# Projections and cluster products of a clustered-attention stage, from one f32 product to three products of f16 parts

## The reference

```python
x = layernorm(inputs, ln1_g, ln1_b)
q = einsum('bsd,dhf->bshf', x, Wq)            # 16 heads of 8 features; k, v alike
qb = softmax(einsum('bshf,hfn->bshn', q, Whq))   # 32 clusters per head; kb alike
kb = softmax(einsum('bshf,hfn->bshn', k, Whk))
logits = einsum('bqhf,bkhf->bhqk', q, k) / sqrt(8)
logits = logits + 0.1 * einsum('bqhn,bkhn->bhqk', qb, kb)
out = einsum('bhqk,bkhf->bqhf', softmax(logits), v)
out = einsum('bqhf,hfd->bqd', out, Wo)
```

## Time and profile before

| what | value |
|---|---|
| median of 3 runs | 1559.28 us (1555.27 to 1565.25) |
| the profiled execution's own time | 1561.78 us |
| span of the profiled execution, first to last instruction | 1559.7 us |
| granted TensorE clock, mean | 0.941 |
| busy share over the span: PE, DVE, ACT, POOL | 84%, 74%, 66%, 50% |

### The profile page before, as it was taken

The page is one execution under the profiler, slowest core; times in us unless marked ns, Lnnn a source line. Parts: engine busy times, 40 slices in busy tenths (PEclk is TensorE's granted clock), DMA queues, the critical chain, the costliest instruction groups (busy, mean ns, idle before and its releaser), DMA issues. The chain is left out here.

```text
span 1559.7 us, 27015 instructions
## 1 busy us (share of the span) xinstructions
PE 1302.9 (84%) x9156; PEld 604.5 (39%) x9156; DVE 1154.4 (74%) x1983; ACT 1032.9 (66%) x2355; POOL 787.6 (50%) x957
## 2 busy tenths in 40 slices
PE   3488989999899886786899999859778999998596
PEld 1122222222222221572555555533235555555243
DVE  5778878888888772234888888859458888887493
ACT  3246666666666665775889999852268899987422
POOL 4567666676675500225767777500077667774000
PEclk9569999999999999897999999979889999999698
DMA  3523333333433300101111111010011111110001
GB/s 97 108 55 62 62 68 62 72 61 58 75 62 63 67 2 1 54 1 38 25 25 27 30 25 25 19 44 0 14 32 25 25 25 25 32 25 12 1 1 55
DMA packets 161259, 60.87 MB, mean 39 GB/s; under 512 B 139706, under 2 KB 152932, under 8 KB 161124
## 3 DMA queue, kind: packets, MB, share of 16 engines
q1 hardware_dynamic: 161124, 59.15, 18.0%
HBM read 8.66 MB, written 2.10 MB: 7 GB/s over the span
## 5 line engine op out<-in xcount | busy, mean ns | idle before, releaser
L633 DVE TENSOR_REDUCE row_max<-max_ps 128x2 f32<-128x1024 f32 x256 | 312.9, 1222 | 71.0 <-PE max_ps L445 69.6
L685 ACT ACTIVATE prob<-scores_ps 128x1024 f32<-128x1024 f32 x256 | 262.0, 1023 | 148.4 <-PE scores_ps L425 144.9
L1668 POOL TENSOR_TENSOR la_turned<-la_raw,lw_rot 128x1024 f32<-128x1024 f32 x64 | 150.7, 2355 | 275.6 <-ACT la_raw L1560 146.0
L1549 ACT ACTIVATE la_s<-la_s,la_bias,la_inv 128x128 f32<-128x128 f32 x512 | 222.9, 442 | 8.2 <-DVE la_bias L1462 7.9
L1305 PE MATMUL la_ring<-lw_wqkv,la_hT 128*128 128x512 f32 x384 | 205.7, 647 | 24.8 <-ACT la_hT L1544 13.4
L425 PE MATMUL scores_ps<-stack 128*128 128x512 f16 x512 | 155.8, 386 | 41.5 <-ACT prob L685 40.8
L1674 POOL TENSOR_TENSOR la_turned<-la_turned,la_swapped 128x1024 f32<-128x1024 f32 x64 | 150.6, 2353 | 5.0
L459 PE MATMUL heads_ps<-prob,v_pad 128*32 128x512 f32 x1024 | 137.3, 608 | 1.1 <-ACT prob L685 1.1
L445 PE MATMUL max_ps<-stack 24*128 24x512 f16 x512 | 102.8, 398 | 31.8 <-DVE row_max L633 19.2
L1437 DVE TENSOR_TENSOR la_swapped<-la_ring,lw_rot 128x256 f32<-128x256 f32 x256 | 92.0, 416 | 32.6 <-ACT la_raw L1560 25.3
L425 PEld LDWEIGHTS scores_ps<-stack 128*128 128x128 f16 x512 | 34.2, 97 | 208.5 <-ACT prob L685 160.8
(11 more groups left out here) (170 smaller groups left out, 2727.3 us busy)
## 6 DMA issues: line engine op xcount, KB each, us to landing
la_v_back<-la_v_own SPq DMA_DIRECT2D x112, 128.0 KB, 2.3
X<-in_x SPq DMA_DIRECT2D x8, 256.0 KB, 5.0
stack<-stack_tok SPq DMA_TRANSPOSE x128, 3.2
out<-X SPq DMA_DIRECT2D x8, 256.0 KB, 2.4
lw_wqkv<-in_wqkv SPq DMA_DIRECT2D x2, 768.0 KB, 4.9
stack<-shift_row SPq DMA_DIRECT2D x64, 2.0 KB
lw_rot<-in_rot SPq DMA_DIRECT2D x2, 512.0 KB, 6.2
lw_w<-in_fw SPq DMA_DIRECT2D x2, 341.0 KB
```

The costliest lines, as they stand in the source:

```text
L633: nc.vector.tensor_reduce(row_max[:, grp % 2, w // 2, :, w % 2], max_ps[:], AX.X, ALU.max).then_inc(max_made, 1)
L685: nc.scalar.activation(prob[:, c % 4, 2 * pr:2 * pr + 2, :], scores_ps[:], ACT.Exp, scale=1.0 / LOGIT_SCALE).then_inc(exp_made, 1)
L1549: ins = nc.scalar.activation(s_ps[:, place(h), :], s_ps[:, place(h), :], ACT.Exp, bias=bias[:, T % 2, h:h + 1], scale=inv[:, T % 4, h:h + ...
L1668: nc.gpsimd.tensor_tensor(spun, raw[:, T % 2].rearrange("p s (h f) -> p s h f", f=LD), rot[:, T % TPB, :, 0, :].unsqueeze(2).to_broadcast( ...
```

## The change

For the 28 tiles after the first batch the three products `qkv`, `clk` and `clq` are made of f16 parts: x_hi W_hi + x_hi W_lo + x_lo W_hi, accumulated in one PSUM bank, in place of one f32 product. What was issued for it:

- once, ScalarE copies `w_qkv` (384 columns) and `w_cl` (1024 columns) to f16, in the slot in which tile 1 is in step 0 (slot -41), ahead of everything else in that slot
- once, VectorE subtracts to get the low parts of both, in the slot in which tile 2 is in step 0 (slot -33), ahead of everything else in that slot
- for each of the 28 tiles, `turn_input` runs a second activation on the same bench region, with f16 output, before the one that writes `xnT`
- for each of them GpSimd subtracts `xnT_hi` from `xnT` (`split_input`, step -5, slot 2 modulo 8), after `scale_input` and ahead of `place_values` and the cluster work of that slot
- TensorE waits for `xnT_split` before each of the products, and once for the low weights

```diff
+            def project(out, x, whole, hi, lo):
+
+                if x < TPB:
+                    return nc.tensor.matmul(out, xnT[:, x % 2, :], whole, start=True, stop=True)
+                pe.wait_ge(xnT_split, x + 1 - TPB)
+                if x == TPB:
+                    pe.wait_ge(w_lo_made, 2)
+                nc.tensor.matmul(out, xnT_hi[:, x % 2, :], hi, start=True, stop=False)
+                nc.tensor.matmul(out, xnT_hi[:, x % 2, :], lo, start=False, stop=False)
+                return nc.tensor.matmul(out, xnT_lo[:, x % 2, :], hi, start=False, stop=True)
...
-                    mm = nc.tensor.matmul(bench[:, 0:3 * D], xnT[:, x % 2, :],
-                                          w_qkv[:].rearrange("p a b -> p (a b)"), start=True, stop=True)
+                    mm = project(bench[:, 0:3 * D], x, flat(w_qkv[:]), w_qkv_hi[:], w_qkv_lo[:])
...
-                    mm = nc.tensor.matmul(bench, xnT[:, x % 2, :], w_cl[:, step == "clk", :],
-                                          start=True, stop=True)
+                    side = int(step == "clk")
+                    mm = project(bench, x, w_cl[:, side, :], w_cl_hi[:, side, :], w_cl_lo[:, side, :])
...
+            def split_weights():
+                dve.wait_ge(w_hi_made, 2)
+                nc.vector.tensor_tensor(w_qkv_lo[:], flat(w_qkv[:]), w_qkv_hi[:], ALU.subtract).then_inc(w_lo_made, 1)
+                nc.vector.tensor_tensor(flat(w_cl_lo[:]), flat(w_cl[:]), flat(w_cl_hi[:]),
+                                        ALU.subtract).then_inc(w_lo_made, 1)
...
+                if tile_at_step(n, 0) == 2:
+                    split_weights()
...
+                if x >= TPB:
+                    nc.scalar.activation(xnT_hi[:, x % 2, :], filled("xn", x)[:, 0:P], ACT.Identity,
+                                         bias=ln1[:, 1:2], scale=ln1[:, 0:1])
...
+                if tile_at_step(n, 0) == 1:
+                    nc.scalar.activation(w_qkv_hi[:], flat(w_qkv[:]), ACT.Copy).then_inc(w_hi_made, 1)
+                    nc.scalar.activation(flat(w_cl_hi[:]), flat(w_cl[:]), ACT.Copy).then_inc(w_hi_made, 1)
...
+            def split_input(x):
+                pool.wait_ge(xnT_made, x + 1)
+                nc.gpsimd.tensor_tensor(xnT_lo[:, x % 2, :], xnT[:, x % 2, :], xnT_hi[:, x % 2, :],
+                                        ALU.subtract).then_inc(xnT_split, 1)
...
+                x = tile_at_step(n, -5)
+                if x is not None and x >= TPB:
+                    split_input(x)
```

More of the change, by code:

```diff
@@ L287, in clustered_attention @@
         w_cl = sb("w_cl", [P, 2, H * NB])
+        w_qkv_hi, w_qkv_lo = sb("w_qkv_hi", [P, 3 * D], F16), sb("w_qkv_lo", [P, 3 * D], F16)
+        w_cl_hi, w_cl_lo = sb("w_cl_hi", [P, 2, H * NB], F16), sb("w_cl_lo", [P, 2, H * NB], F16)
         w_o = sb("w_o", [P, D])
@@ L291, in clustered_attention @@
         xnT = sb("xnT", [P, 2, P])
+        xnT_hi, xnT_lo = sb("xnT_hi", [P, 2, P], F16), sb("xnT_lo", [P, 2, P], F16)
         qkv = sb("qkv", [P, 2, 3, D])
@@ L337, in clustered_attention @@
         xn_made = sem("xn_made")
-        xnT_made = sem("xnT_made")
+        xnT_made, xnT_split = sem("xnT_made"), sem("xnT_split")
+        w_hi_made, w_lo_made = sem("w_hi_made"), sem("w_lo_made")
         qkv_made = sem("qkv_made")
```

## The result

The changed kernel took 1573.6 us (median, 1572.7 to 1574.0, four runs) against 1558.4 (1555.3 to 1565.3) for the kernel before on the same chip: a ratio of 1.0091, interval 1.0057 to 1.0125. I had forecast 1557.6 and a range of 1548 to 1567. It is slower, and outside the range.

What follows compares the result with a forecast made beforehand. The stage was taken as a balance of four rings, not bound by TensorE alone. Products less second activation -2.0, weights +1.8, lower clock -1.5 sum to -1.7 us: 1560.1 profiled, 1557.6 as median, range 1548 to 1567.

Steps and rivals of the forecast that it cites:

- the wait for GpSimd in slot 2: Slot 2: VectorE waits 0.91 us for GpSimd's part of the cluster sum, covering the added activation in three tiles of four.
- the test of the prediction: Sign expected in the profile after: in the usual tile VectorE's wait for GpSimd in slot 2 stays.
- The one that ended slower: Rival: ScalarE's added activation in slot 0 is uncovered, 0.34 us per tile, 9.5 in all, giving 1566.6 us; chance 12%.
- within 1%: Whole kernel: chance 0.87 of a time within 1% of before, against 0.08 faster and 0.05 slower.
- from max scores to scores across a cluster product: Attention stage, sign expected where TensorE binds: this distance becomes 1.07 us in place of 1.28.
- The median batch: Attention stage at full clock: each batch gains between 0.2 and 0.5 us, products less the added activation.
- the second activation: ScalarE, slot 0: delays the exponential 0.34 us per tile, passed on only in the second tile of each batch.
- The products: Attention stage at full clock: shorter products let through 0.09 to 0.18 us per tile, another 0.2 at the turned heads.
- The weight loads: TensorE products: loads of 97 ns taken as hidden; the rival that they are exposed gives 1567 us, chance 4%.
- the first rival: Attention stage: TensorE binds after all, so the whole 16.4 us come out, giving 1543.2 us; chance 12%.
- The prologue: Before the stage: ScalarE's copies and VectorE's subtractions of the weights cost +0.9 to +3.1 us, taken as +1.8.
- What would make it wrong: Attention stage: VectorE's wait for GpSimd shrinks with the cycle, or the clock falls where it was full as TensorE does less.

Runs made afterwards that it cites:

- experiment 12: The kernel before with only the second activation added, into a buffer nobody reads: 1562.79 us, ratio 1.0003.
- experiment 4: The changed kernel without second activation or GpSimd subtraction, the third product taking the high part again: 1571.87 us, ratio 1.0078 against the kernel before.
- the overheads together: The changed kernel with all f16 parts made but unused, TensorE running the f32 product without new waits: 1565.01 us, ratio 1.0040 against the kernel before.
- keys first: Second key-side transposing transfer issued before the first query-side one: kernel before 1555.45 us (0.9957), changed kernel 1555.92 (0.9950), ratios against the kernel before in its old order.
- displaced by 32: The kernel before with 64 already satisfied waits (32 instructions) at the head of TensorE's list: 1568.35 us, ratio 1.0048.
- displaced by 64: The kernel before with 128 already satisfied waits (64 instructions) at the head of TensorE's list: 1579.23 us, ratio 1.0121.

## Why the prediction was wrong

**The step that failed** is the wait for GpSimd in slot 2, which the forecast took over from the trace of before. The sentence that "the GpSimd part for which VectorE waits 0.91 us follows from transfers that are issued before `clq` is due" took the landing of the transfers as fixed once their issue was. In the usual tile the wait did stay, as the test of the prediction had it: of the 23 such waits between 162 and 560 us the median is 0.91 us before and 1.00 after. But in five tiles of the changed kernel it is 1.7 to 2.9 us, and over the stage it grew from 21.5 to 31.1, because transfers issued at the same place landed up to 5.0 us later. The sum had no term for what a changed count of TensorE's instructions does to the place of the program fetches. That term is worth about +12 us (15.1 less 3.3 above the medians). Without it the span would have grown by 11.2 less 11.8, so -0.6, where -1.7 was forecast; with one profile of each kernel, and runs of the kernel before that spread over 10 us, so close an agreement is partly luck.

No rival named it either. The one that ended slower had the right direction, but +7.3 for the 15.2 us between the medians of the runs, and the wrong mechanism. That the kernel would stay within 1% had been given 0.87; it did (0.91%, interval up to 1.25%), but through a loss that the prediction didn't know, so that is luck.

**A term mis-sized:** from max scores to scores across a cluster product I gave 1.07 us after 1.28. The changed kernel has 305.78 - 304.80 = 0.98:

```profile
304.80 0.39 PE L449 MATMUL max_ps<-stack 24*128 24x512 f16 x2
...
305.12 0.39 PE L476 MATMUL bench<-w_cl_hi,xnT_hi 128*128 128x512 f16 x1
...
305.35 0.38 PE L477 MATMUL bench<-w_cl_lo,xnT_hi 128*128 128x512 f16 x1
...
305.56 0.38 PE L478 MATMUL bench<-w_cl_hi,xnT_lo 128*128 128x512 f16 x1
...
305.78 0.59 PE L429 MATMUL scores_ps<-stack 128*128 128x512 f16 x2
```

I had charged the two max scores 0.43 us by the rate of two score products. Here the next product starts 0.32 after them. The f32 product so had 0.96 of the 1.28, not 0.85; three f16 products take 0.66 (0.23, 0.21, 0.22). That is 0.30 saved each and not 0.21. It changed little, because TensorE is ahead of the other rings there.

**What held, with its sizes.** The median batch: forecast -0.2 to -0.5 us, measured -0.03. Taken apart, the second activation was to pass 0.34 on once per batch, and alone it costs 0.38 (experiment 12). The products were to bring 0.56 to 0.83 (0.09 to 0.18 in three tiles, 0.09 in the fourth, 0.2 at the turned heads), and alone bring 0.39 (experiment 4). So less seems to get through of each product than I worked out, although each saves more, and the small gain of -2.0 in the sum is nil. These sizes are rough: displacing a kernel alone moved its median batch by 0.2 us (65.43 to 65.60, 65.40 to 65.21), and the overheads together, the activation among them, gave 0.26. In the cycle the exponential of slot 1 comes 2.63 us after that of slot 0, for 2.29 before, as forecast (2.6 and 2.3). The changed kernel's `xnT` stands 0.34 behind the new activation and the exponential 0.35 behind that:

```profile
312.49 0.45 ACT L713 ACTIVATE xnT_hi<-bench,ln 128x128 f16<-128x128 f32 x1
312.83 0.46 ACT L715 ACTIVATE xnT<-bench,ln 128x128 f32<-128x128 f32 x1
313.18 1.03 ACT L707 ACTIVATE prob<-scores_ps 128x1024 f32<-128x1024 f32 x1
```

The weight loads are hidden: three products start 0.23 and 0.21 apart, each with a load of its own of 95 to 99 ns. The rule of the Trainium skill that was weighed ("TensorE: Matmul & The Clock Gate", Part 3) would have them exposed, and the trace contradicts it for these products too. TensorE did less and the kernel gained nothing, so the first rival, that TensorE binds, is false.

**The prologue** came out as forecast in kind. ScalarE's copies move the exponential from 32.58 to 33.82, +1.24 for +1.2; VectorE's subtraction of `w_cl` takes 1.76 us for 1024 columns, above the 1.20 that was its share of my 1.65:

```profile
33.82 0.61 ACT L743 ACTIVATE cl<-cl 128x512 f32<-128x512 f32 x1
...
41.81 1.76 DVE L653 TENSOR_TENSOR w_cl_lo<-w_cl,w_cl_hi 128x1024 f16<-128x1024 f32 x1
```

The first row maximum is at 73.4 for 72.1, inside the 1 to 3 us, and made up for by the first exponential (96.1 for 96.6; forecast +1.8 and -1.5). That the shorter products at the lower clock paid for it fits, but is not shown: the displaced copies of the kernel before have 96.2 and 97.2 there.

**What would make it wrong** did name the lower clock, but as a result of TensorE doing less. The stretches at 369.4 and 488.9 came right behind stalls. With keys first neither the kernel before nor the changed one has any in the stage up to 600 us; kernels without a hit can have the one near 533 all the same, the activation alone for 10.2 us.

**Left open.** Late landings go with the transfers of q8 in 54 of 66 cases; why one of 16 KB adds 1.5 us and more to transposing transfers was not measured. That the queue serves TensorE is inferred from the count, and from the displacement of TensorE's list alone, which moves its transfers. Which engine q14 serves is not known. A version with the change and the old instruction count per tile wasn't tried. The program behind the stage takes 945 to 952 us in these profiles whatever was changed in the stage; that spread goes into every ratio. It is 952 for the kernel before displaced by 32 and 950 displaced by 64, for 945 undisplaced; whether fetches do the same there was not looked into.

## What to carry to other kernels

Adding or removing TensorE's instructions moved where its program is fetched here, and with it where other transfers are disturbed. That alone cost up to 1.2%, so before a difference of 1% is put down to an edit, run a copy of each kernel with its program displaced by a few dozen satisfied waits, and look at the sum above the median cycle, not only at the mean. Where a ring waits for a transfer with less than a microsecond to spare, put the awaited transfer first in its queue: that made both kernels 0.4 to 0.5% faster than the kernel before, and left the disturbance only in the first tile of a batch. Compare the median cycle of two traces first; if it is the same, look for stalls and what they have in common.

## What the runs showed of the hardware that I had not expected

- A 16 KB transfer on the instruction queue q8, once per 253 records of TensorE, goes with transposing transfers that land after 4.7 us at the median and 5.5 at most, for 3.2 and 3.6 without one.
- 64 added instructions that do nothing, at the head of TensorE's list, cost 20 us of 1559.
- Two f16 max-score products let the next product start 0.32 us after them, two score products 0.43.
- 512 columns of an f32 product cost 0.96 us of TensorE in place (301.02 to 301.98), the three f16 products 0.66.
- After a wait of 1.84 us TensorE had the lower clock for 3.4 us in the largest stall, in which the scores took 1.06 us in place of 0.59.
